# The drain of a fused decoder layer on Trainium2: second PSUM banks for three projections, an earlier normalisation, and one product moved from GpSimd to VectorE

## The reference

```python
x = _layernorm(x + _L0_attn_ref(x, ...))             # 16 heads of 64, biases on q, k, v and out
x = _layernorm(x + _L0_xattn_ref(ctx, ctx, x, mask, ...))  # one head of 64, integer mask
x = _layernorm(x + _L0_ffn_ref(x, ...))              # 32 experts, top 8, capacity 512, silu(gate) * up
```

## Time and profile before

| | us |
|---|---|
| median of 3 runs | 1905.0 (1904.68 to 1906.51) |
| profiled execution: time | 1901.5 |
| profiled execution: span | 1899.8 |
| TensorE busy | 1812.9 (95%) |
| GpSimd busy | 1215.7 (64%) |
| VectorE busy | 1177.0 (62%) |
| ScalarE busy | 979.9 (52%) |

### The profile page before, as it was taken

How to read it: one execution, slowest core, us unless ns; L and a number is a source line. 1 busy time by engine, 2 the same in 40 slices (tenths; PEclk the granted TensorE clock), 3 DMA queues, 4 the chain that set the end, 5 groups by cost and what they waited for, 6 DMA issues and landing times. The chain is left out here.

```text
span 1899.8 us, 43319 instructions
## 1 busy us (share of the span) xinstructions
PE 1812.9 (95%) x15536; PEld 1081.0 (57%) x15536; DVE 1177.0 (62%) x2183; ACT 979.9 (52%) x1972; POOL 1215.7 (64%) x1006
## 2 busy tenths in 40 slices
PE   7999999999999999999997789999999999999991
PEld 4676676677667776777675444444444444444440
DVE  5556777777777777787777754444444444444464
ACT  7766666676567666665764323333333333333334
POOL 4766766876687667766776145656666655565545
PEclk9999999999999999999998899999999999999996
DMA  8766776576656655766567469999999999999986
GB/s 245 151 129 119 140 138 143 112 155 138 138 115 152 144 133 109 157 145 137 103 148 150 156 187 254 235 242 235 241 235 234 246 236 237 240 242 233 236 263 260
DMA packets 609454, 347.26 MB, mean 183 GB/s; under 512 B 515312, under 2 KB 537840, under 8 KB 607344
## 3 DMA queue, kind: packets, MB, share of 16 engines
q1 hardware_dynamic: 580000, 273.04, 60.2%
q0 software_dynamic: 29392, 73.42, 16.8%
HBM read 160.77 MB, written 61.34 MB: 117 GB/s over the span
## 5 line engine op out<-in xcount | busy, mean ns | idle before, releaser
L724 PE MATMUL bank<-arena_x,arena_wo 128*128 128x256 f16 (+1 forms) x4224 | 608.2, 302 | 9.2 <-ACT qk L1250 5.3
L724 PEld LDWEIGHTS bank<-arena_x,arena_wo 128*128 128x128 f16 x4224 | 407.3, 98 | 196.4 <-issue 10.7
L2426 POOL TENSOR_TENSOR arena_p<-arena_p 128x512 f16<-128x512 f32 x256 | 329.2, 1308 | 100.1 <-ACT arena_p L1269 100.1
L2646 POOL DMA_INDIRECT acc_rows<-arena_wo,cur_to x120 | 235.6, 1963 | 227.4 <-ACT arena_wo L1613 199.9
L1668 DVE SCALAR_TENSOR_TENSOR arena_wo<-stage,arena_wo 128x1536 f16<-128x1536 f32 (+3 forms) x77 | 175.9, 2290 | 293.5 <-ACT arena_wo L1337 280.3
L1194 PE MATMUL bank<-arena_wo 128*128 128x512 f16 x1152 | 254.0, 379 | 0.2 <-DVE arena_wo L2331 0.2
L724 PE MATMUL bank<-arena_v,arena_wo 128*128 128x512 f16 x1152 | 251.3, 379 | 0.8 <-DVE arena_v L2015 0.8
L2421 POOL TENSOR_TENSOR qk<-qk 128x512 f16<-128x512 f32 x128 | 161.9, 1265 | 111.2 <-ACT qk L1250 110.9
L1260 ACT ACTIVATE arena_p<-bank,s_neg 128x256 f32<-128x256 f32 x512 | 203.3, 504 | 15.1 <-DVE s_neg L1702 12.6
L1248 ACT ACTIVATE qk<-bank,bqkv 128x256 f32<-128x256 f32 x256 | 123.2, 481 | 149.6 <-PE bank L724 148.9
L1613 ACT ACTIVATE arena_wo<-bank,cur_w 128x512 f32<-128x512 f32 x120 | 74.5, 686 | 239.1 <-PE bank L1194 239.1
(11 more groups left out here) (211 smaller groups left out, 2360.9 us busy)
## 6 DMA issues: line engine op xcount, KB each, us to landing
stage<-wguT SPq DMA_DIRECT2D x31, 1536.0 KB, 8.3
stage<-wdnT SPq DMA_DIRECT2D x31, 768.0 KB, 11.9
arena_x<-xT SPq DMA_DIRECT2D x16, 512.0 KB, 4.1
arena_r<-x_rows SPq DMA_DIRECT2D x16, 512.0 KB, 5.0
stage<-ctxT SPq DMA_DIRECT2D x16, 512.0 KB, 4.3
x_rows<-arena_r SPq DMA_DIRECT2D x16, 512.0 KB, 3.0
acc_rows<-arena_r SPq DMA_DIRECT2D x16, 512.0 KB, 3.3
stage<-arena_p SPq DMA_TRANSPOSE x256, 3.3
```

The source lines that it names most:

```text
L724: mm = pe.matmul(out_ap, lhs(a, i), rhs(c, i), start=(n == 0 and i == 0), stop=(n == 2 and i == chunks - 1))
L2426: gp.tensor_tensor(halves[:, j % 2, h, 1, :], probs[:, j % 2, h].rearrange("p t k -> p (t k)"), halves[:, j % 2, h, 0, :], ALU.subtract).t ...
L2646: gp.indirect_dma_start(acc_rows, bass.IndirectOffsetOnAxis(ap=cur_to[:, k, c:c + 1], axis=0), y[:, k, c, :], None, compute_op=ALU.add).th ...
```

## The change

1. `cross_project(b, 1)` of batches 14 and 15 writes another bank than `cross_project(b, 0)`: bank 2 and bank 5. It waits for both low halves of x1T instead of for the read of the first half.
2. `project(15, 1)` writes bank 4 and waits for the last exponentials of the self attention instead of for the read of the first half.
3. On VectorE `norm1(B - 1)` comes before `kv2_lo(B - 1)`.
4. The product of batch 14's probabilities with the reciprocals goes from GpSimd to VectorE, directly behind the reciprocals.

```diff
+        def cross_out_bank(b, t):
+            if t and last_but_one(b):
+                return bank[2]
+            if t and last(b):
+                return bank[5]
+            return cross_bank(b)
+
+        def project_bank(b, t):
+            return bank[4] if t and last(b) else ps_v
...
                         pe.wait_ge(x1t_lo, count(b - 1, TT, 1))
+                elif last(b):
+                    pe.wait_ge(e_done, 2 * B * EC)
                 else:
                     pe.wait_ge(ln1, count(b, 7, t))
-                split_mm(ps_v[:, :], lambda a, i: oT[:, i // 2, 4 * (i % 2) + 2 * a + t, :],
+                split_mm(project_bank(b, t)[:, :], lambda a, i: oT[:, i // 2, 4 * (i % 2) + 2 * a + t, :],
...
                     pe.wait_ge(o2_lo, count(b, 1, 1))
+                elif last(b) or last_but_one(b):
+                    pe.wait_ge(x1t_lo, count(b, TT, TT))
                 else:
                     pe.wait_ge(ln2, count(b, 7, t))
...
-            def normalise_last():
-                row_scales2(B - 1)
-                dve.wait_ge(r2_done, B)
+            def normalise(b):
+                row_scales2(b)
+                dve.wait_ge(r2_done, count(b, 1, 1))
...
                 heads_out(B - 1, 7)
-                row_scales2(B - 2)
+                normalise(B - 2)
                 split_ctx(B - 1)
...
                 add_slots(B - 3)
+                norm1(B - 1)
                 kv2_lo(B - 1)
-                norm1(B - 1)
                 x1_lo(B - 1, 0)
...
                 heads_parts(B - 1, 5)
-                normalise2(B - 2)
                 heads_parts(B - 1, 7)
```

More of the change, by code:

```diff
@@ L879, in cross_project @@
                 pe.wait_ge(s_const, N_CONST)
-                split_mm(cross_bank(b)[:, :], lambda a, i: o2[:, a, t * P:(t + 1) * P], lambda c, i: wxo[:, c, :], 1)\
+                split_mm(cross_out_bank(b, t)[:, :], lambda a, i: o2[:, a, t * P:(t + 1) * P], lambda c, i: wxo[:, c, :], 1)\
                     .then_inc(out2_mm, 1)
@@ L1735, in residual1 @@
                     past(dve, ln2, count(b, 7))
-                vec.scalar_tensor_tensor(out=z[:, t, :], in0=ps_v[:, :], scalar=1.0 / W_SCALE, in1=xr[:, t, :],
+                vec.scalar_tensor_tensor(out=z[:, t, :], in0=project_bank(b, t)[:, :], scalar=1.0 / W_SCALE, in1=xr[:, t, :],
                                          op0=ALU.mult, op1=ALU.add).then_inc(ln1, 1)
@@ L1815, in residual2 @@
                     dve.wait_ge(x1b_done, count(b, 1, 1))
-                vec.scalar_tensor_tensor(out=first_rows(b)[:, t, :], in0=cross_bank(b)[:, :], scalar=1.0 / W_SCALE, in1=z[:, t, :],
+                vec.scalar_tensor_tensor(out=first_rows(b)[:, t, :], in0=cross_out_bank(b, t)[:, :], scalar=1.0 / W_SCALE, in1=z[:, t, :],
                                          op0=ALU.mult, op1=ALU.add).then_inc(ln2, 1)
@@ L2273, in drain @@
                 low_part(B - 2, 0)
-                normalise_last()
+                normalise(B - 1)
                 low_part(B - 2, 1).then_inc(rt, 1)
```

## The result

The changed kernel takes **1899.72 us** (median of 8 runs, 1899.06 to 1902.08) beside 1906.23 us for the kernel before (8 runs on the same chip, 1904.34 to 1909.65). The ratio is 0.9965 with a 95% interval of 0.9957 to 0.9974: 6.5 us less, between 5.0 and 8.2. The forecast was 3.2 us less and 1901.8 us, within 1900.0 to 1904.3.

What follows compares the result with a forecast made beforehand. Experts keep TensorE busy without gap, so only the drain's way to the first expert at 1113.15 counts. 2.9 us with the old clock plus 0.3 us from a smaller gap made 3.2 us: 1905.0 to 1901.8 us, range 1900.0 to 1904.3.

Steps and rivals of the forecast that it cites:

- Bank 5: Batch 15's second cross projection: VectorE was busy until 0.04 us after the result, so worth 0 to 0.05 us, taken as 0.
- the added 1.24 us are worth half at full speed: Batch 15's first projection starts 1.24 us earlier but, with the clock's rise unmoved near 1047.6, ends only 0.62 us earlier.
- the steps on the two second banks: Batch 14's second cross projection, 0.62 us after the clock; batch 15's second projection, 0.79 us wait and 0.15 us overlap gone.
- 0.25 us for batch 14's product: Batch 14's product on VectorE: turn 0.39 us earlier, of which 0.25 us stays behind the context's low half.
- the normalisation and what lies behind: Normalisation ahead of the keys' low halves in batch 15: turn of x1 at 1061.15, 2.94 us earlier.
- the cap of 2.9 us by the two transposes: Batch 14's router product needs two DMA transposes, the second landing near 1062.8, which cuts the gain to about 2.9 us.
- clock higher: Rival: denser TensorE work from 1042 to 1063 us raises the clock; together 4.4 to 5 us, about 1900.4 us; chance 0.33.
- the rival's 1.2 us: Query product and scores behind the turn of x1 at full speed: each saves 0.6, up to 1.2 us.
- GpSimd first: Rival: GpSimd's cast runs before VectorE's batch 14 product, turned low half 0.85 us late; 2.5 us gain, 1902.5 us; chance 0.12.
- The gain does not arrive: Rival: a later transfer or VectorE's table work sets the first expert's start, swallowing 2 to 3 us; 1904.5 us; chance 0.06.
- slower: Rival: clock stays at 1.2 GHz through both batch 15 projections; 5.7 us slower, 1910.7 us; chance 0.06 with smaller mishaps.

Runs made afterwards that it cites:

- e12: The changed kernel without bank 5 and with 40 filler matmuls ahead of the first gather in place of 24: 1900.64 us, ratio 0.9970.
- e6: The changed kernel without bank 5, batch 15's second cross projection writing bank 6 and waiting for the first half's read: 1903.95 us, ratio 0.9981.
- e5: The changed kernel again, with no edit: 1900.84 us, ratio 0.9965.
- e11: The changed kernel with 40 filler matmuls ahead of the first gather in place of 24: 1898.87 us, ratio 0.9954.
- e1: The kernel before again, with no edit, as a control: 1906.33 us, ratio 0.9996.
- e2: The kernel before with only `norm1(B - 1)` moved ahead of `kv2_lo(B - 1)`: 1906.40 us, ratio 0.9999.
- e4: The kernel before with only batch 14's product moved from GpSimd to VectorE: 1906.09 us, ratio 0.9994.
- e9: The kernel before with 40 filler matmuls ahead of the first gather in place of 24: 1905.72 us, ratio 0.9996.
- e10: The kernel before with `norm1(B - 1)` ahead of `kv2_lo(B - 1)` and 40 filler matmuls ahead of the first gather in place of 24: 1904.56 us, ratio 0.9983.
- e15: The kernel before with more fillers: 8 for 4 before batch 14's turn of probabilities, 8 new before x1's turn, 40 before the first gather: 1906.24 us, ratio 0.9994.
- e8: The changed kernel with batch 14's product on GpSimd again: 1902.64 us, ratio 0.9975.
- e14: The changed kernel with batch 14's product on GpSimd again and 40 filler matmuls ahead of the first gather in place of 24: 1901.02 us, ratio 0.9964.
- e16: The changed kernel with 18 fillers instead of 10 ahead of the last turn and 40 ahead of the first gather: 1899.17 us, ratio 0.9955.

## Why the prediction was right in kind and wrong in size

**Right: the waits.** Each place named came out as written: the product at 0.69 us and first against GpSimd's cast, 0.95 us from the reciprocal's start to the turn (within 1.0 was asked); both 0.79 us of idle time gone; the second residual bound by VectorE's queue; 3.88 us from it to the turn of x1 (1.84 less than before, 1.61 forecast); the router product not late. Bank 5 was given 0 to 0.05 us. From batch 15's turn of probabilities to its last turn it is 9.80 us after and 9.86 before, and in both the two residuals follow each other at VectorE's pace; e12's trace agrees (9.87 us). That was worked out for a second cross projection at full speed. At the low level, in e6, VectorE waits for it, and bank 5 is worth 0.6 us. The means of two comparisons, 2.7 us (e6 against e5) and 2.3 us (e12 against e11) with 2.0 and 2.2 of uncertainty, have more, and no trace shows where it would lie. What bank 5 buys beyond 0.6 us stays open.

**Wrong: "the added 1.24 us are worth half at full speed".** This was the step on batch 14's second cross projection. It held the clock's rise fixed at 1047.6, 8.8 us behind the turn of batch 14's probabilities, while the work moved. The rise did not stay: it came 7.7 us behind the turn in the changed kernel, 7.1 to 9.2 (mean 8.2) in all eleven profiles that have these banks, and 8.8 to 11.0 (mean 10.0) in the six without them (before, e1, e2, e4, e9, e10; e15 with its fillers aside). The ranges overlap, so this holds for the means and not for each execution: in e8 and e12, with the banks, it came 9.2 us behind the turn, later than in the first profile of the kernel before. On the mean the gain was not halved, it grew. From the first cross projection to the place table the six take 15.7 to 16.7 us (mean 16.1), the eleven 13.1 to 14.5 (mean 13.9): 2.3 us, where the steps on the two second banks had 1.3. The waits and the overlap behind them, taken at full value, are 1.9 us. For the start of the first projection the forecast had 1.24 us and 2.14 were measured, because it also left the clock out of what lies ahead: the product of the probabilities with v ran in 0.52 us and not 0.85, and the first of the six cross products ran at the high level.

**Too small: 0.25 us for batch 14's product.** The step read GpSimd's 1.04 us off one profile and took it for the rule. In five of ten profiles it is 1.94 to 1.96 us, and the turn 0.9 us later. That such a pair of instructions exclude one another was in the prediction, but only as a danger to the product in its new place; that it already struck in the old one was missed. The pair of profiles above does not show it, and the measured times do contain it.

**Wrong by less: the normalisation and what lies behind.** From place table to turn of x1 the forecast had 1.37 us (2.94 less 1.57) and 1.65 came, since the cap of 2.9 us by the two transposes did not bind: counted from the reciprocal they were issued 1.9 us earlier than before, as SP's queue of the changed kernel shows, and the router product at 1066.50 had no idle time before it.

```profile
1061.52 2.95 SPq L525 DMA_TRANSPOSE stage<-arena_r  x2
```

Behind the turn of x1 another 0.7 us came (4.50 against 5.24 us), 0.26 of it before batch 15's turn of probabilities, where the second low stretch shrank from 10.3 to 6.8 us. The rival *clock higher*, at 0.33, came near in its price (4.4 to 5 us; the pair of profiles has 4.5 to 5.2), but only in half of its mechanism. The clock did rise earlier against the work. It fell again all the same, at 1068.8, and the query product and the scores, on which the rival's 1.2 us rested, took 1.49 and 1.46 us as before (TensorE at 1068.94 and 1071.37). So that match is in part luck. The low level took 26.9 to 30.8 us of the stretch in all kernels with one of the parts or none (e15 with its fillers aside), and 20.3 to 23.8 in the whole; by e15 such a difference need not be a gain by itself.

**The sum.** The first pair of profiles gives 4.5 us by the drain and 5.2 from the reciprocal. The mean of before and e1 less that of the change and e5 gives 5.6 and 5.8, and e9 less e11 gives 6.7 and 6.3 (of these, 1.3 us are the collision and lie ahead of the turn). The fit has 6.1, the direct comparison 6.5 (5.0 to 8.2). So the traces leave nothing over; the first pair was merely one without the collision. The forecast also stood on a median of three runs, 1905.0; eight gave 1906.23. From that the same 3.2 us would have led to 1903.0, so the reference hid 1.2 us of the error. The clock in the first 52 us is no part of the change, but it moves single executions by up to 5 us and is one reason why parts worth 1 to 2 us need many runs.

*GpSimd first*: on VectorE the product started 0.03 us ahead of GpSimd's cast and won. The Trainium skill, "SBUF — State Buffer", Who interferes with whom, lets the first to start win; the trace agrees in that the product kept its 0.69 us, while GpSimd's subtraction behind, beside VectorE's low half of the context, took 1.95 us in place of 1.15 (e14), and in that GpSimd's product of e8, started second, took 1.96 in place of 1.04. *The gain does not arrive* and *slower* did not happen: the 4.5 us gained up to the turn of x1 reached the first expert, with 0.7 more.

## What to carry to other kernels

Where work before a clock step is moved up, do not hold the step fixed: here it moved by 1.8 us on the mean, so price the gain in full and make the halved value the lower bound, not the middle. Before pricing an instruction from one profile, look whether a neighbour on another engine may start ahead of it in the next: here that nearly doubled its time in half of the profiles. Filling idle time with dummy matmuls bought nothing here, in e15 and e16: another engine set the pace, and at the low level the fillers held up the work behind them. Compare profiled executions from the last common point ahead of the change, and price parts of 1 to 2 us only by many runs, taken out of the whole as well as put in alone.

## What the runs showed of the hardware

TensorE's granted clock in the first 52 us differed between executions of the same code there (0.97 and 0.87, and 303 or 241 matmuls done), which shifts the rounds by up to 5 us. VectorE's operation on 128x1024 with two inputs in SBUF, started 0.15 to 0.16 us ahead of GpSimd's product of 128x512, lengthened that product from 1.04 us to 1.94 or 1.96; which of the two started first differed between executions and kernels. A gap of 4.2 to 4.6 us before the first gather's transposes brought a low stretch of either 3.2 to 3.6 or 10.3 us; the long one reaches some 4 us into the expert and costs 1.7 to 2.0 us (17.45 to 17.70 against 15.71 us for 72 matmuls), and with 40 filler matmuls in the gap it was absent in all eight profiles.
